# A graph network on one core: scatter with one product a tile instead of two, messages doubled and masked

## What is computed

```python
# layer 0, gated: z = [h[dst], h[src], edge_attr]
m = sigmoid(z @ W_f + b_f) * softplus(z @ W_s + b_s) * exp(-d**2 / 18)
out = segment_sum(m, dst) + h
# layer 1, plain: z = [h[src], h[dst], edge_weight1]
out = segment_sum(relu(z @ W1 + b1) @ W2 + b2, dst)
# layer 2: two GATv2 attention layers of 5 heads (self loops added)
a = softmax over the edges of a node; out = segment_sum(a * xl[src], dst).mean(heads) + bias
# layer 3, copied: out = elu(batchnorm((segment_sum((h / sqrt(deg_out))[src], dst) / sqrt(deg_in)) @ W + b))
```

## Time and profile before

| | |
|---|---|
| runs | 5562.61 us median of 3 (5561.23 to 5564.41) |
| the profiled execution | 5557.08 us, span 5555.0 us |
| granted TensorE clock, mean | 0.871 |
| PE, PEld busy | 4095.7 us (74%), 3075.3 (55%) |
| DVE, ACT, POOL busy | 3270.0 (59%), 2967.9 (53%), 3265.0 (59%) |
| DMA | 680.39 MB, mean 122 GB/s |

### The profile page before, as it was taken

The page is one execution under the profiler, slowest core; times in us unless marked ns, Lnnn a source line. Parts: engine busy times, 40 slices in busy tenths (PEclk is TensorE's granted clock), DMA queues, the critical chain, the costliest instruction groups (busy, mean ns, idle before and its releaser), DMA issues. The chain is left out here.

```text
span 5555.0 us, 125887 instructions
## 1 busy us (share of the span) xinstructions
PE 4095.7 (74%) x31967; PEld 3075.3 (55%) x31967; DVE 3270.0 (59%) x7378; ACT 2967.9 (53%) x7228; POOL 3265.0 (59%) x3335
## 2 busy tenths in 40 slices
PE   1079996499961999975997679999299894155574
PEld 0068885487751666653773256666177552155552
DVE  3945557588876333337879943333688799622266
ACT  0268885466655555534872234555288324755547
POOL 0876662377732655525878965554188687677710
PEclk6589998799985999987999989999699997577785
DMA  9477774755547555541334455555133334622224
GB/s 256 87 168 179 179 180 101 155 155 154 152 121 204 123 120 120 120 98 53 121 106 95 95 132 120 120 121 122 33 121 121 90 92 96 142 78 79 79 65 145
DMA packets 1204167, 680.39 MB, mean 122 GB/s; under 512 B 625921, under 2 KB 1100477, under 8 KB 1202266
## 3 DMA queue, kind: packets, MB, share of 16 engines
q1 hardware_dynamic: 1039724, 532.72, 37.1%
q0 software_dynamic: 63360, 65.01, 7.0%
q10 hardware_dynamic: 100948, 81.22, 4.6%
HBM read 379.93 MB, written 298.10 MB: 122 GB/s over the span
## 5 line engine op out<-in xcount | busy, mean ns | idle before, releaser
L1989 DVE COPY zT_l<-zTp_l 128x512 f32<-128x512 f32 x196 | 135.5, 691 | 899.6 <-PE alp_l L1907 650.8
L933 ACT ACTIVATE hot_e<-iota_n,rel 128x256 f32<-128x256 f32 x980 | 422.8, 499 | 418.3 <-PE part_e L956 412.4
L973 DVE TENSOR_TENSOR acc<-acc,part_e 128x128 f32 x1176 | 335.2, 285 | 467.5 <-PE part_e L956 341.7
L1964 ACT ACTIVATE leak_l<-tp_l,bcat 128x512 f32<-128x512 f32 x588 | 375.9, 686 | 433.0 <-PE tp_l L1919 404.0
L956 PE MATMUL part_e<-z_e,hot_e 128*128 128x128 f32 x1568 | 282.4, 354 | 384.0 <-DVE acc L1687 187.0
L1059 POOL DMA_INDIRECT z_l<-h_d,src_i x392 | 384.1, 980 | 288.2 <-PE zTp_l L1100 192.1
L1059 POOL DMA_INDIRECT z_l<-g_d,src_i x392 | 384.6, 981 | 287.1 <-PE zTp_l L1100 190.9
L1969 ACT ACTIVATE leak_l<-tp_l,bcat 128x256 f32<-128x256 f32 x784 | 307.7, 476 | 345.1 <-PE tp_l L1926 345.1
L1059 POOL DMA_INDIRECT z_e<-h_d,src_i x392 | 377.9, 964 | 183.8 <-issue 96.8
L956 PEld LDWEIGHTS part_e<-z_e,hot_e 128*128 128x128 f32 x1568 | 260.2, 259 | 406.1 <-DVE acc L1687 187.2
L1195 POOL DMA_INDIRECT z_e<-h_d,row_of_e x392 | 384.7, 981 | 124.6 <-issue 113.1
(11 more groups left out here) (419 smaller groups left out, 11050.9 us busy)
## 6 DMA issues: line engine op xcount, KB each, us to landing
m_d<-m_e ACTq DMA_DIRECT2D x196, 256.0 KB, 2.2
m_d<-m_m SPq DMA_DIRECT2D x196, 256.0 KB
h_d<-h SPq DMA_DIRECT2D x56, 448.0 KB
relb_e<-rel_d SPq DMA_DIRECT2D x196, 128.0 KB
near_e<-h_d SPq DMA_DIRECT2D x392, 64.0 KB
near_e<-g_d SPq DMA_DIRECT2D x392, 64.0 KB
relb_l<-rel_d SPq DMA_DIRECT2D x196, 128.0 KB, 3.4
near_l<-h_d SPq DMA_DIRECT2D x392, 64.0 KB
```

The source lines that it names most:

```text
L933: ins = self.nc.scalar.activation(self.hots[k][:, t, :], self.S["iota_n"][:, :], ACT.Abs, scale=-1.0, bias=self.S["rel"][:, ds(n * BLK + t ...
L973: ins = self.nc.vector.tensor_tensor(x, x, part[:, t % 2, :, 0:x.shape[2]], ALU.add)
L1964: nc.scalar.activation(leak[u % 2][:, q, :], tp[q][:, :], ACT.Relu, bias=bcat[:, 0, q:q + 1], scale=1.0 - SLOPE).then_inc(leak_ready, 1)
```

## The change

A tile's edges are multiplied once. `part_of` (new, made in setup) holds for each edge two numbers, one for each of the two node tiles, 1 for the one its target lies in and 0 for the other, and `rel` is reduced to 0 to 127. The message is written twice side by side, each copy times its number of `part_of` (`split`), and one product of the 128-wide one-hot with the doubled message gives both tiles' sums. The doubling is `pick` on VectorE, and `pick_too` on ScalarE for the last tiles. One-hots are 128 wide. VectorE's `match` is one instruction for all its tiles. `hots` is a ring of `deep` buffers (four; two in gated_edges), `split` a ring of two.

- message stages: both VectorE and ScalarE make two of a block's four one-hots and two of its four doublings. VectorE's body: pick n-2, weigh n, match n, add n-3.
- gated_edges: pick n-2 on VectorE after match n-1. All four doublings of a block on VectorE here and in the next two.
- plain_edges: ScalarE copies the message out of PSUM, the bias comes by a product (`b1b3`), VectorE picks. The second add for the in-degree is gone; a column of ones in the messages of the first message stage gives it, which makes them 70 wide (`AW`), and the first `attention_nodes` copies it to `deg_in`.
- copied_edges: `pick` n, then add n-1; GpSimd waits for `picked`; the clearing covers 393 x 64 columns.
- messages and `m_d` have their real width (64, 70, 69) instead of 128.
- setup: two comparisons and one combination for `part_of` and `rel`, and the split of a second bias in three. `iota_b`, `square`, `diff_i` go; `finish` keeps its output tiles in `acc`.

```diff
     def hot(self, act, n, u):
+        hot = self.hots[u % self.deep]
+        need(act, self.summed, BLK * (n - self.deep + 1))
         for t in range(self.on_act):
-            ins = self.nc.scalar.activation(self.hots[k][:, t, :], self.S["iota_n"][:, :], ACT.Abs, scale=-1.0,
+            ins = self.nc.scalar.activation(hot[:, t, :], self.S["iota_n"][:, 0:P], ACT.Abs, scale=-1.0,
                                             bias=self.S["rel"][:, ds(n * BLK + t, 1)])
...
+    def match(self, dve, n, u):
+        count = BLK - self.on_act
+        need(dve, self.summed, BLK * (n - self.deep + 1))
+        self.nc.vector.tensor_tensor(self.hots[u % self.deep][:, self.on_act:BLK, :], wide(self.S["iota_n"][:, 0:P], 1, count),
+                                     wide(self.S["rel"][:, ds(n * BLK + self.on_act, count)], 2, P), ALU.is_equal).then_inc(self.matched, 1)
+
+    def pick(self, dve, n, u, m):
+        tiles = slice(0, self.picked_first)
         need(dve, self.summed, BLK * (n - 1))
+        self.nc.vector.tensor_tensor(self.split[u % 2][:, tiles, :, :], wide(m[:, tiles, :], 2, WIN),
+                                     wide(self.S["part_of"][:, ds(n * BLK, self.picked_first), :], 3, self.width), ALU.mult).then_inc(self.picked, 1)
+
+    def pick_too(self, act, n, u, m):
+        need(act, self.summed, BLK * (n - 1))
+        for t in range(self.picked_first, BLK):
+            for w in range(WIN):
+                ins = self.nc.scalar.activation(self.split[u % 2][:, t, w, :], m[:, t, :], ACT.Copy, scale=self.S["part_of"][:, ds(n * BLK + t, 1), w])
+        ins.then_inc(self.picked_too, 1)
 
     def multiply(self, pe, n, u):
         need(pe, self.hot_ready, n + 1)
+        pe.wait_ge(self.picked, n + 1)
         for t in range(BLK):
             if t % 2 == 0:
                 need(pe, self.added, BLK * (n - 1) + t + 2)
             if t == self.on_act:
                 need(pe, self.matched, n + 1)
-            for w in range(WIN):
-                mm = self.nc.tensor.matmul(self.parts[t // 2][:, t % 2, w, :], self.hots[k][:, t, w * P:(w + 1) * P], m[:, t, :],
-                                           start=True, stop=True)
+            if t == self.picked_first:
+                pe.wait_ge(self.picked_too, n + 1)
+            mm = self.nc.tensor.matmul(self.parts[t // 2][:, t % 2, :, 0:self.width], self.hots[u % self.deep][:, t, :], self.split[u % 2][:, t, :, :],
+                                       start=True, stop=True)
...
 def attention_messages(nc, S, g):
+        sums = NodeSums(nc, S, ctx, name, WIDTH, on_act=2, picks_on_act=2)
...
             def _(act):
                 def body(n, u, i):
-                    sums.hot(act, n, u % 2)
-                    need(act, sums.summed, BLK * (n - RINGS + 1))
+                    if has(n, 2):
+                        pick(n - 2, u + UN - 2)
+                    sums.hot(act, n, u)
+                    need(act, sums.picked, n - RINGS + 1)
...
             def _(dve):
                 def body(n, u, i):
+                    if has(n, 2):
+                        pick(n - 2, u + UN - 2)
                     weigh(n, u)
-                    if has(n, 2):
-                        sums.add(dve, n - 2, sums.windows(dve, n - 2))
+                    sums.match(dve, n, u)
+                    if has(n, 3):
+                        sums.add(dve, n - 3, sums.windows(dve, n - 3))
```

More of the change, by code:

```diff
@@ L972, in add @@
             x = self.sums_to[:, ds(los[t], WIN), :]
-            ins = self.nc.vector.tensor_tensor(x, x, part[:, t % 2, :, 0:x.shape[2]], ALU.add)
-            if self.more is not None:
-                y = self.more[:, ds(los[t], WIN), :]
-                ins = self.nc.vector.tensor_tensor(y, y, part[:, t % 2, :, C:self.width], ALU.add)
-            ins.then_inc(self.added, 1)
+            self.nc.vector.tensor_tensor(x, x, part[:, t % 2, :, 0:self.width], ALU.add).then_inc(self.added, 1)
 class NearRows:
@@ L1318, in body @@
                     if has(n, 2):
-                        scatter(n - 2, u + UN - 2)
+                        sums.multiply(pe, n - 2, u + UN - 2)
                     project(n, u)
@@ L1322, in _ @@
                 for n in range(NB - 2, NB):
-                    scatter(n, n)
+                    sums.multiply(pe, n, n)
             @block.scalar
@@ L1571, in body @@
                     nc.scalar.activation(uT[k][:, :], uTp[k][:, 0:2 * P], ACT.Relu, bias=S["b1"][:, 0:1]).then_inc(uT_ready, 1)
+                    if has(n, 1):
+                        take(n - 1, u + UN - 1, i + (u - 1) // RINGS)
                     if has(n, 2):
@@ L1574, in _ @@
                 blocks(act, body)
-                sums.hot(act, NB - 1, 1)
+                sums.hot(act, NB - 1, NB - 1)
+                take(NB - 1, NB - 1, (NB - 1) // RINGS)
                 for n in range(NB - 2, NB):
@@ L1771, in body @@
                         x = sums_to[:, ds(b[k], WIN), :]
-                        ins = nc.vector.tensor_tensor(x, x, part[k][:, :, 0:x.shape[2]], ALU.add)
-                        if more is not None:
-                            y = more[:, ds(b[k], WIN), :]
-                            ins = nc.vector.tensor_tensor(y, y, part[k][:, :, C:width], ALU.add)
-                        ins.then_inc(added[k], 1)
+                        nc.vector.tensor_tensor(x, x, part[k][:, :, :], ALU.add).then_inc(added[k], 1)
                     dve.wait_ge(added[RING - 1], i + 1)
@@ L2244, in _ @@
                 blocks(act, body)
+                for n in range(NB - 2, NB):
+                    pick(n, n)
             @block.vector
```

254 lines of the change are left out of this document (135 added, 119 removed).

## The result

The changed kernel takes 6204.5 us (median of 4 runs, 6201.8 to 6205.0), the kernel before 5561.9 (median of 4): ratio 1.1154, 95% interval 1.1135 to 1.1173. Forecast were 5944 us, in a range of 5800 to 6080: slower was right, but 643 us were lost where 381 had been forecast, and the time lies above the range.

The account below looks back on a forecast made before the run. The prediction took a message-stage loop through VectorE's adds and TensorE's projection to bound the changed kernel: +427 - 26 + 0 - 23 + 3 = +381 us, giving 5944 us, range 5800 to 6080.

Parts of the forecast that it names:

- the loop: Message stages: last add, scatter's second pair, projection, weighing, one-hots, adds close once a block; 5.05 us, 6.6 at low clock.
- the signs that the prediction named: Right: message period 5 to 5.8 us, VectorE and TensorE waiting, lower clock; wrong: among others gated_edges above 5.8 a block.
- a mean of .87 over the two levels ... is 26% of the time low: Message stages: TensorE's clock, taken from node_tables, lengthens the block from 5.05 to 5.45 us; both stages +427 us.
- The high end of the range: Message stages: 5.8 us a block, with TensorE's clock as in copied_edges (.75); +68 us on 5944.
- the 46 us that the other stages were to gain: Outside the message stages: gated_edges -26, plain_edges 0, copied_edges -23, setup +3 us.
- Rival C: Message stages: GpSimd's first addition gets the shared ports before VectorE's one-hots; 6.3 to 6.6 a block, about 6140 us; chance .07.
- Rival A: Message stages: VectorE alone bounds them; 3.85 a block plus .3 for GpSimd, 4.15, +175, total 5690 us; chance .09.
- The multiply loses .96: gated_edges: eight fewer scatter instructions at .12 each give back .96 us of the two-block chain.
- The chain: gated_edges: dependencies across engines over two blocks, 11.64 us, falling to 11.10, 5.55 a block; -26 us.
- plain_edges: +1.0 for 0: plain_edges: GpSimd's gathers stay at 5.08 us a block; 0, ends -20 and +20.
- the pace of the gathers before: copied_edges: gathers of .944 us plus .231 issue time, 90.5/392; 376 at 1.20 after the clearing; stage -23 us.
- setup: +4.9 for +3: Setup: splitting a second bias adds 13 chained small instructions of about .23 us; +3 us.

Follow-up runs that it names:

- b_add3: Kernel before, with VectorE in both message stages adding the sums of block n-3 instead of n-2; ratio to before 1.112, message stages 681 and 676 us.
- m_add2: Changed kernel, with VectorE in both message stages adding the sums of block n-2 instead of n-3; ratio to before 1.029, 4.22 us a block.
- m_filler: Changed kernel plus six useless TensorE products after each projection in both message stages; ratio to before 1.061, message stages 534 and 526 us.
- m_hots_act: Changed kernel, message stages adding block n-2 and with all four one-hots on ScalarE; ratio to before 1.018, 3.95 and 3.94 us a block.
- after_again: Changed kernel, nothing edited, measured again in a later group; ratio to before 1.104, message stages 666 and 658 us.

## Why the prediction was wrong

In short: the loop was found, its length at both clocks was right, and the mix of the two clocks was not. Of the signs that the prediction named, VectorE's wait for the projection, TensorE's for the adds and the lower clock are there, while the period of 6.5 us lies outside 5 to 5.8 and gated_edges, at 5.85 a block, shows one of the signs of being wrong.

- **Message stages, the mechanism: right.** The loop from the last add over the second pair and the projection behind it closes once a block. b_add3 makes it in the kernel before with one line, m_add2 takes it out with one line.
- **Message stages, the size: the step that failed is the clock** ("a mean of .87 over the two levels ... is 26% of the time low"). The loop at full clock was 5.05 in the sum and 5.20 and 5.15 in m_filler; at the low clock it was 6.6 in the sum, and 6.57 and 6.50 in the trace at a mean of .57. The two ends were sized well, each a little short. The mix between them was not: .40 a block was added for the clock, and it was 1.35. TensorE was granted .57, which by the same reckoning is low for 86% of the time: 5.05 + .86 x 1.55 = 6.38, and 6.53 from the 5.20 of m_filler. I had taken .87 from the busy share of node_tables, but that share is measured at whatever clock was granted, and a slow product is busy for longer: in the stage of the changed kernel TensorE is busy 415 of 610 us, 68%, and still at .57, while in m_add2 246 of 390, 63%, stand beside .95. The high end of the range was drawn the same way (copied_edges, 5.8 a block) and not from the loop's own low-clock sum of 6.6, which the text had worked out; that end would have put the top of the range at 5562 + 194 x (6.6 - 3.25) = 6212, or 6166 with the 46 us that the other stages were to gain and did not.
- **Rival C** (6140) was nearest in time and wrong in cause: the one-hots are .42 long and go ahead of GpSimd's addition, as forecast, and b_add3 has the same pace without them.
- **Rival A** is what is left when the loop is opened: 4.22 for 4.15. Its .3 for GpSimd is near what VectorE loses at the port there: from the end of the adds to the end of the doubling are .80 in the mean in m_add2, where the doubling alone lasts .45.
- **gated_edges: +5.5 for -26.** The step that failed is "The multiply loses .96". Before, the first pair's eight instructions covered the second pair of adds; four don't, and TensorE waits. The chain by the measured terms: 11.64 - .45 - .18 + .65 = 11.66, 5.83 a block, no gain; the measured pace is 5.85. That these terms make it is read from the trace; the runs that were to test it stayed inconclusive, so this cause is argued and not shown.
- **plain_edges: +1.0 for 0,** right; GpSimd's gathers set it.
- **copied_edges: -5.2 for -23.** The step that failed is the pace of the gathers before: I divided 90.5 us of issue time by 392 gathers, but the row gives it for 297 of them, .305 each. A gather came every 1.25 us before and comes every 1.25 us now; there was nothing to win back beyond the start. The seventeenth gather starts 6.9 us earlier in the stage: the clearing begins 2.1 earlier and is 1.6 shorter, and the other 3.2 are that GpSimd waits for the first doubling instead of the first block's products. Some 2 us of that are lost again later.
- **setup: +4.9 for +3:** not resolved by one profile. The same setup took 145.6 to 151.4 us in the ten profiles that have it, and the old one 145.2 and 145.5 in two.

## What to carry to other kernels

When a step is moved back by one iteration in one engine's queue, follow every counter that it raises into the other queues, with what stands behind the waiting instruction there: a loop that spanned two iterations can close over one, and no engine's busy time tells of it. A busy share taken at a lowered TensorE clock is no measure of TensorE's work; size a new stage at both clock levels and let the range reach to the slower one when the engine will stand idle each iteration. A group's idle time has its own count beside it, and the mean is taken by that count. When a stage is slow, compare the time from issue to landing before blaming the transfers: here the landings had not moved.

## What the runs showed of the hardware

- More work on TensorE made the kernel faster: with 1.78 us of useless products a block the granted clock went from .57 to 1.00 and the stages from 667 to 534 us. With the same work in a block of 4.22 us it was .95 and .82 (m_add2). The slow loop and the low clock fed each other.
- GpSimd's 512-wide addition lasts 1376 ns in the middle when it starts inside a 256-wide VectorE instruction of two SBUF tensors and 1272 without it. VectorE's 280-wide doubling lasts .45 us by itself and takes .88 from the adds before it in the mean when GpSimd adds without a pause (m_hots_act).
- One program's edge stages differed by 9 to 19% between two measurements (after and after_again: gated_edges 607 and 662 us, plain_edges 547 and 652, copied_edges 506 and 598), while its message stages repeated to .2%. The logits stages, which gather too, moved by 4% (729 and 731 to 759 and 760 us). The gathers landed as soon after their issue in both.
